# Routed attention of four batches in 32-row groups, in a two-layer language tower on one core

## The reference

```python
scores = sigmoid(normed @ Wr + br)
k = max(1, int(round(0.15 * l)))               # 19 of 128 tokens of a batch
_, idx = top_k(-scores, k)
attn_mask = zeros((b, l), bool).at[arange(b)[:, None], idx].set(True)
...                                            # 12-head attention of all tokens
attn_out = ctx @ Wo + bo
...
merged = where(attn_mask[..., None], attn_out, mix_out)
h = hidden_states + merged
```

## Time and profile before

| | |
|---|---|
| time, median of 3 runs | 887.48 us (884.51 to 888.21) |
| span of the profiled execution | 888.4 us |
| PE busy | 722.9 us (81%), 5500 instructions |
| DVE busy | 519.8 us (59%), 1760 instructions |
| ACT busy | 302.3 us (34%) |
| POOL busy | 245.1 us (28%) |
| chain that ended last, by engine | PE 61%, DVE 18%, issue 6%, POOL 4%, ACT 4%, DMA 3% |
| mean granted clock of TensorE | 0.931 of full speed |

### The profile page before, as it was taken

The page is one execution under the profiler, slowest core; times in us unless marked ns, Lnnn a source line. Parts: engine busy times, 40 slices in busy tenths (PEclk is TensorE's granted clock), DMA queues, the critical chain, the costliest instruction groups (busy, mean ns, idle before and its releaser), DMA issues.

```text
span 888.4 us, 15579 instructions
## 1 busy us (share of the span) xinstructions
PE 722.9 (81%) x5500; PEld 545.4 (61%) x5501; DVE 519.8 (59%) x1760; ACT 302.3 (34%) x688; POOL 245.1 (28%) x304
## 2 busy tenths in 40 slices
PE   1888778988777998858798967768868879999993
PEld 1546355566556665647656645745447878988892
DVE  7458677865678774668887367871253443333330
ACT  0133241634333253433353433421334323333330
POOL 5322200470013244001445201330001533333332
PEclk9999899999968999998999997889897989999997
DMA  7950000000001000000111000048001323222220
GB/s 249 412 237 2 0 1 1 19 7 2 1 1 37 23 17 4 2 1 1 54 19 8 1 3 1 25 173 284 0 2 31 63 49 46 36 36 38 36 35 8
DMA packets 29894, 43.63 MB, mean 49 GB/s; under 512 B 5355, under 2 KB 24597, under 8 KB 29830
## 3 DMA queue, kind: packets, MB, share of 16 engines
q1 hardware_dynamic: 19250, 30.87, 10.1%
q0 software_dynamic: 8752, 9.07, 6.3%
q10 hardware_dynamic: 1828, 2.84, 0.9%
HBM read 21.36 MB, written 22.09 MB: 49 GB/s over the span
## 4 chain that ended last, share of the span: by engine, by line
PE 61%; DVE 18%; issue 6%; POOL 4%; ACT 4%; DMA 3%; another core or an unknown queue 1%; ACTq 1%; SPq 1%; DVEq 0%; POOLq 0%
PE qa L1840 26%; PE qc L1840 25%; PE qa L1843 5%; PE qc L1843 4%; DMA out<-qk_T 2%; DVE mx L1435 2%; POOL arena_w L440 1%; DMA mu_row<-in_mu 1%; DVE st L1042 1%; POOL rs_a L475 1%; ACTq L633 1%; DVE arena_e L1256 1%; DVE qk_T L1441 1%; DVE xb L1059 1%
## 5 line engine op out<-in xcount | busy, mean ns | idle before, releaser
L1840 PE MATMUL qc<-arena_w,big 128*128 x468 | 83.1, 328 | 1.4 <-DVE qk_T L1819 1.4
L1840 PE MATMUL qa<-arena_b 128*128 128x128 f32 (+2 forms) x688 | 75.1, 293 | 9.7 <-ACT arena_b L763 4.9
L1840 PEld LDWEIGHTS qa<-arena_b 128*128 128x128 f32 (+2 forms) x688 | 66.1, 195 | 19.4 <-issue 7.5
L1840 PEld LDWEIGHTS qc<-arena_w,big 128*128 128x128 f32 x468 | 75.6, 191 | 2.1 <-issue 2.0
L1008 ACT ACTIVATE big<-qa,arena_b 128x128 f32<-128x128 f32 x156 | 43.1, 375 | 80.8 <-PE qc L1840 66.9
L1840 PE MATMUL qa<-arena_e,nT 128*128 128x192 f32 (+2 forms) x256 | 69.9, 429 | 0.4 <-ACT nT L671 0.3
L1808 DVE COPY arena_b<-qc 128x256 f32<-128x256 f32 x39 | 16.6, 426 | 90.6 <-PE qc L1843 79.6
L603 POOL DMA_INDIRECT out<-qk_T x39 | 61.1, 1566 | 21.0 <-POOL spare L602 10.6
L1840 PEld LDWEIGHTS qa<-arena_e,nT 128*128 128x128 f32 x256 | 47.0, 198 | 22.0 <-issue 12.3
L475 POOL TENSOR_TENSOR rs_a<-rs_a,minus_half 128x4 f32<-128x4 f32 x8 | 8.1, 1012 | 177.5 <-DVE rs_a L1055 170.1
L479 POOL TENSOR_TENSOR rs_b<-rs_b,minus_half 128x4 f32<-128x4 f32 x12 | 12.5, 1042 | 152.3 <-DVE rs_b L1055 152.3
(11 more groups left out here) (368 smaller groups left out, 1592.0 us busy)
## 6 DMA issues: line engine op xcount, KB each, us to landing
slots<-xk SPq DMA_DIRECT2D x1, 13192.0 KB, 43.1
arena_e<-in_w SPq DMA_DIRECT2D x8, 579.0 KB, 7.9
arena_w<-in_w SPq DMA_DIRECT2D x8, 576.0 KB, 9.0
qk_T<-slots SPq DMA_DIRECT2D x39, 97.0 KB, 1.9
out<-hb SPq DMA_DIRECT2D x16, 96.0 KB
arena_e<-in_w_l SPq DMA_DIRECT2D x1, 804.0 KB
arena_e<-in_W ACTq DMA_DIRECT2D x1, 768.0 KB
out<-qk_T POOLq DMA_INDIRECT x39
```

What stands on the lines that cost most here:

```text
L1840: return nc.tensor.matmul(o, l, r, start=start, stop=stop)
```

## The change

The 19 selected tokens of the four batches are laid side by side, each padded to a group of 32 (KP = 32), so that the four batches fill 128 rows.

```diff
-        pw = sb("pw", [128, G, KSEL + 1])
+        pw = sb("pw", [128, G, KP])
-        ctxT = sb("ctxT", [KR, C, G, KSEL])
+        ctxT = sb("ctxT", [KR, C, G, KP])
+        def attn_of(b):
+            return QA[:, (b + 2) % G, 0:D]
...
             def pselT_evac(ta):
-                w(ta, "pselT_p", 4)
-                A(pselT[:, :, :].rearrange("p b t -> p (b t)"), PA[0:KSEL, 0, :], ACT.Copy).then_inc(*done("pselT"))
+                w(ta, "pselT_p", 1)
+                A(pselT, PA[:, 0, 0:128], ACT.Copy).then_inc(*done("pselT"))
-            def asel_evac(ta, hf):
-                w(ta, "asel_p", 2 * hf + 2)
-                A(aselb[:, 2 * hf:2 * hf + 2, :].rearrange("p b n -> p (b n)"), PB[0:KSEL, hf, 0:2 * D], ACT.Copy).then_inc(*done("asel"))
+            def asel_evac(ta):
+                w(ta, "asel_p", 1)
+                A(aselb, PB[:, 0, 0:D], ACT.Copy).then_inc(*done("asel"))
...
-            step(fill(ctxT[CW:KR, :, :, :], 0.0))
+            step(fill(ctxT[:, :, :, :], 0.0))
+            step(fill(pw[:, :, :], 0.0))
...
             def contexts(ta, hf):
-                for b in (2 * hf, 2 * hf + 1):
-                    w(ta, "ctx", half(b))
-                    T(ctxm[:, :, b, :].rearrange("p c (h k) -> p c h k", h=HC),
-                      half_of(PB, CW, b // 2, HC * KSEL)[:, b % 2, :, :].rearrange("p c (h k) -> p c h k", h=HC),
-                      bc(bc(hmb, 2, KSEL), 1, C), ALU.mult).then_inc(s["ctx_m"], 1)
-                    w(ta, "ctx_m", b + 1)
-                    nc.vector.reduce_sum(ctxT[0:CW, :, b, :], ctxm[:, :, b, :].rearrange("p c (h k) -> p c k h", h=HC),
-                                         AX.X).then_inc(s["ctxT"], 1)
+                two = slice(2 * hf, 2 * hf + 2)
+                w(ta, "ctx", 2 * hf + 2)
+                T(ctxm[:, two, :, :].rearrange("p b c (h k) -> p (b c) h k", h=HC),
+                  half_of(PB, CW, hf, HC * KSEL).rearrange("p b c (h k) -> p (b c) h k", h=HC),
+                  bc(bc(hmb, 2, KSEL), 1, 2 * C), ALU.mult).then_inc(s["ctx_m"], 1)
+                w(ta, "ctx_m", hf + 1)
+                nc.vector.reduce_sum(ctxT[0:CW, :, two, 0:KSEL].rearrange("p c b k -> p b c k"),
+                                     ctxm[:, two, :, :].rearrange("p b c (h k) -> p b c k h", h=HC), AX.X).then_inc(s["ctxT"], 1)
             def selected_in(ta, hf):
                 for b in (2 * hf, 2 * hf + 1):
-                    w(ta, "attn", half(b))
+                    w(ta, "attn", b + 1)
                     w(ta, "hin", b + 1)
-                    T(x[:, b, :], x[:, b, :], psl(PB, b, D), ALU.add).then_inc(s["hin"], 1)
+                    T(x[:, b, :], x[:, b, :], attn_of(b), ALU.add).then_inc(s["hin"], 1)
...
             def x1_T(ta, hf):
-                since(pe, s["hin"], ta * PER["hin"] + (2 * hf - 2))
+                since(pe, s["hin"], ta * PER["hin"] + (hf - 3))
             def proj(ta, b):
                 w(ta, "xT", 1 if b == 0 else 2)
+                if b == 0:
+                    since(pe, s["hin"], ta * PER["hin"])
...
             def select_T(ta):
                 w(ta, "rank", 20)
-                for b in range(G):
-                    inc(tr(PA[0:KSEL, 0, tok(b)], pw[:, b, 0:KSEL], 128), "pselT_p")
+                inc(tr(PA[:, 0, 0:128], pw[:, :, :].rearrange("p b k -> p (b k)"), 128), "pselT_p")
...
-            def selected(ta, hf):
-                w(ta, "ctxT", 2 * hf + 2)
-                for b in (2 * hf, 2 * hf + 1):
-                    inc(both(psl(PB, b, D)[0:KSEL, :], lambda c: ctxT[:, c, b, :], lambda c: w_fo[:, c, :]), "asel_p")
-            def attn(ta, hf):
-                w(ta, "asel", hf + 1)
-                for b in (2 * hf, 2 * hf + 1):
-                    inc(mm(psl(PB, b, D), pselT[:, b, :], aselb[:, b, :]), "attn")
+            def selected(ta):
+                w(ta, "ctxT", 2)
+                inc(both(PB[:, 0, 0:D], lambda c: ctxT[:, c, :, :].rearrange("p b k -> p (b k)"), lambda c: w_fo[:, c, :]), "asel_p")
+            def attn(ta):
+                w(ta, "hin", G)
+                w(ta, "asel", 1)
+                for b in range(G):
+                    rows_ = slice(KP * b, KP * b + KSEL)
+                    inc(mm(attn_of(b), pselT[rows_, :], aselb[rows_, :]), "attn")
```

More of the change, by code:

```diff
@@ L30 @@
 KSEL = max(1, int(round(0.15 * S)))
+KP = 32
 NE = 8
@@ L71 @@
     ln2=15, ln3=7, zdot=4, zexp=1, score=7, n3T=4, nT=2, dg=4, bc=4, ssum=1, bcs=1, rank=22,
-    sel=4, selT=2, qT=1, q_bias=2, kT=1, kT_evac=2, v2p=4, v2=2, pselT_p=4, pselT=1, lg=4, nmax=8,
-    pexp=8, pnorm=12, pT_p=4, pT=2, ctx=4, ctx_m=4, ctxT=4, asel_p=4, asel=2, attn=4, mixT=8, mix=4, hin=8, hb=8,
+    sel=4, selT=2, qT=1, q_bias=2, kT=1, kT_evac=2, v2p=4, v2=2, pselT_p=1, pselT=1, lg=4, nmax=8,
+    pexp=8, pnorm=12, pT_p=4, pT=2, ctx=4, ctx_m=2, ctxT=2, asel_p=1, asel=1, attn=4, mixT=8, mix=4, hin=8, hb=8,
     ln4=15, n4T=4, n2T=2, up=6, gelu=6, down=4, h_ffn=4,
@@ L159, in build @@
         qbd = part(arena_w, over, [C, G, HC * KSEL], CW)
-        ctxm = part(arena_w, over, [C, G, HC * KSEL], CW)
-        aselb = part(arena_w, over, [G, D], KSEL)
-        pselT = part(arena_w, over, [G, 128], KSEL)
+        ctxm = part(arena_w, over, [G, C, HC * KSEL], CW)
+        aselb = part(arena_w, over, [D])
+        pselT = part(arena_w, over, [128])
         assert over[0] <= at[0]
@@ L343, in build @@
         KC = (97, 96)
-        V_EMPTY, V_TAU = 2, 25
-        V_MQK, V_UM = 26, 27
-        V_SETUP = 39
+        V_EMPTY, V_TAU = 2, 26
+        V_MQK, V_UM = 27, 28
+        V_SETUP = 40
         R_EARLY, R_DONE = 23, 43
@@ L869, in front @@
                 pT_evac(ta, 1)
-                asel_evac(ta, 0)
-                asel_evac(ta, 1)
+                asel_evac(ta)
             def joint(ta, tb):
@@ L1992, in select @@
                     for c in range(C):
-                        i = mm(PA[0:CW, c, lo:lo + KSEL + 1], xn[:, b, c * CW:(c + 1) * CW], pw[:, b, :])
+                        i = mm(PA[0:CW, c, lo:lo + KSEL + 1], xn[:, b, c * CW:(c + 1) * CW], pw[:, b, 0:KSEL + 1])
                     inc(i, "sel")
@@ L2235, in front @@
                 context(ta, 1)
-                selected(ta, 0)
-                selected(ta, 1)
-                attn(ta, 0)
-                attn(ta, 1)
+                selected(ta)
+                attn(ta)
             def joint(ta, tb):
```

## The result

| | before | after |
|---|---|---|
| median, us (lowest to highest, runs) | 887.21 (884.35 to 888.21, 6) | 890.2 (889.74 to 891.71, 6) |
| ratio after/before, 95% interval | | 1.0047 [1.0034, 1.006] |
| span of the profiled execution, us | 888.4 | 887.9 |
| mean granted clock in it | 0.931 | 0.911 |

The changed kernel is 0.47% slower, 3.0 us between these medians, and the forecast of 885.2 with its range up to 889.0 missed it. The two profiled spans seem to say the opposite. In every run whose span is known the time is the span plus 1.8 to 1.9 us, so the profile of before came from a long execution (its time would be 890.3). The kernel before ran 98 times more beside the experiments, in four rounds with medians of 886.15 to 886.98, at a clock of 0.923 to 0.932 (one more run, of 1109.12 us, is left out).

What follows compares the result with a forecast made beforehand. At the ends of the front and turns, VectorE was taken as nearly the bound. Savings of 1.2 + 0.95 + 0.77 + 0.46 = 3.4 us, less 1.1 for a clock fall, gave net 2.3: 885.2 us, range 881.8 to 889.0.

Steps and rivals of the forecast that it cites:

- The sum: Savings at the four ends before any clock loss: 1.2 + 0.95 + 0.77 + 0.46 = 3.4 us (2.3 to 4.5).
- The back products: Four products spreading contexts back over tokens; even run serially they were in time under VectorE's work, so overlap costed at nothing.
- C: End of a turn at about 444 us; saving 0.46 + 0.31 = 0.77 us.
- at B, C and D only the second pair counts: At these ends a quicker first mask pair only waits for TensorE, so only the second pair's 0.27 us saving counts.
- B: End of a turn at about 298 us, TensorE at its lower clock; saving taken as 0.95 us (0.6 to 1.1).
- D: Turn 3 into the back, about 590 us; saving 0.46 us only, since the statistics need all of x.
- A: Front into turn 1, about 148 us; saving 0.18 + 0.5 + 0.53 = 1.2 us.
- I expect a fall at C that was not there, price 1.1; A and B keep theirs.: TensorE's clock falls newly at C, costing 1.1 us; the low stretches at A and B stay as they were.
- The third rival: Projections at A, B and C start and stay at low clock, costing 4.85 us: 889.0, chance 0.15.
- The kind clock: C stays at full clock, turn 1's low time shortens by a third: 3.4 + 1.6 = 5.0 us, 882.5, chance 0.25.
- No gain: Slow reduction and late back products leave `selected_in` unmoved; 1.1 us saved less 0.6 for clock: 887.0, chance 0.15.
- The reading against the median: Whole kernel: profiled span 888.4 us against median 887.48, called slow by 0.9; forecast 886.1 on the span, 885.2 against median.

Runs made afterwards that it cites:

- e1: The changed kernel with unread TensorE products in three gaps at the end of the front and of each turn; 886.38 us, ratio to before 0.9992.
- e5: The kernel before with no edit, run again for a second profile; profiled span 884.1 us, clock 0.929.
- e11: e3 with unread products: three behind the last context product, a half one behind the Wo product and behind the back products; 882.96 us, ratio 0.9967.
- e2: The kernel before with only the two-batch masks and reductions, its TensorE work unchanged; 883.77 us, ratio 0.9977.
- e12: e1 with three unread products instead of two behind the last context product; 886.29 us, ratio 0.9988.
- e3: The changed kernel with masks and reductions of one batch each, as before, TensorE part of the change kept; 904.46 us, ratio 1.0204.
- e6: e1 with more unread products in each joint turn: one ahead of the queries, two ahead of the mix; 884.16 us, ratio 0.9984.
- e8: The changed kernel with unread products in one place only, two behind the last context product; 886.71 us, ratio 1.0009.
- e9: e2 with unread products in each joint turn: one ahead of the queries, two ahead of the mix; 885.77 us, ratio 0.999.

## Why the prediction was wrong

**The sum is borne out as far as it can be seen.** The forecast's sum of 3.4 us before any clock stands against 3.5 at equal low time, which is good to a us or two. Its terms: mask 0.62 to 0.63 (taken 0.62), reduction 0.92 to 0.93 (taken 0.93), evacuation 0.33 (bound 0.48), the Wo product 0.92 at full clock (taken 0.78). The back products overlap almost fully, 0.61 us for eight where one row group took 1.56, and at full clock they are hidden, as costed. C was put at 0.77 and measures 0.9 (7.4 to 6.5). The first mask pair may count too: "at B, C and D only the second pair counts" rested on the extra 1.3 us of lag of one execution. The shares of A, B and D were not measured singly. The forecast's working for B reads 3.94 us as the sixteen product instructions "and attn"; the row is the sixteen alone, and the 0.25 each is right for them.

**The step that failed** is "I expect a fall at C that was not there, price 1.1; A and B keep theirs." The fall at C came, with the mechanism named. The term of 1.1 us was mis-sized: the runs show 32 us of extra low time, which is some 7.4 us at 0.23 per us (6.7 to 9.3 at 0.21 to 0.29), though not all of it can be laid to the thinned stretch: with the gaps filled 9 to 10 us of it stay. Three things in that sentence were wrong.

- Where: it comes at every end. The chain has 12.94, 12.19 and 13.11 for the three projections. B had no standing fall to keep: its low `context(1)` (1.48) is in one of five profiles with the TensorE work of before. A has one in three of the five (12.18, 12.50, 12.50 against 10.80 twice), so "keeps" was fair for A, though the fall grew there.
- How long: I priced the stretch of the projections alone. The trace of after has these stretches at the low level around the ends (start + length, us; the last column is the whole profile), beside both profiles of before and e1:

```text
          A            B            C                          D             all
before    147.2+3.4    290.6+3.4    none                       591.0+10.2    125.3
e5        133.4+6.8    none         none                       594.2+10.2    128.2
after     145.4+6.8    295.6+6.8    435.5+3.4, 445.7+10.2      595.9+13.7    161.0
e1        none         none         none                       590.6+10.2    134.7
```

  Of the 32.8 us that after has more than e5, 23.9 stand in this table; most of the other 9 lie earlier in the turns. Those and the one at 435.5, which is over before `context(1)` of C, are not in the thinned stretch, and no run ties them to it.

- Through what: the low level reaches the short chain itself. At C the Wo product, the back products and the transposes take 0.73, 0.41 and 0.86 us more than in e1, and the cover of the back products, costed at nothing, is gone: VectorE waits 1.01 for them.

**The third rival** ("the clock turns on the change") is the one that came true in mechanism, with all three ends low. It was under-sized in low time: 15.5 us of extra low time, the difference between two turns of one execution, where 32 came. Its price of 0.31 per us was somewhat high (0.21 to 0.29 between kernels, 0.25 within before). It gave 889.0 with a chance of 0.15; with 32 us at 0.23 on the forecast's 3.4 it gives 887.5 - 3.4 + 7.4 = 891.5, and 890.2 was measured. What should have raised its chance stood in the working: some 2.3 us taken out of 3.83 busy in 4.25, in the one stretch where nothing else can run, and the same edit at all four ends.

The section "HAM oscillation — how this bites in real kernels" of the Trainium skill (TensorE: Matmul & The Clock Gate) says that bursts between idle gaps each start cold; I weighed it down because in the trace of before only the thin stretch at A was followed by a low clock. For the changed kernel's ends the trace agrees in kind (0.62 and 13.11 at C). The waits in its example are longer than the 1.68 us that TensorE idled here at most in that stretch, and the clock fell all the same.

**The kind clock** (882.5) did not come with this kernel, but e11 and e2 reach about that, with 124.2 and 122.5 us of low time. Its sum takes a third of the 4.85 us between the turns (1.6); a third of turn 1's low time, as its text has it, is 10 us (0.10 x 2 x 150.42 / 3), which at 0.31 gives 3.1 and 881.0. **No gain** (887.0) is not borne out: `selected_in` starts 4.8 us behind the end of `context(1)` in e1 and 5.4 in e5, and the filled kernels are faster at equal low time; in after the gain is there and is outweighed.

**The reading against the median** was wrong in its base. The profile was called slow by 0.9 us; by its span it was slow by 3 to 4 against typical runs. The scale of net gains was kept, so this moved the number little, but it is where the low clock of B and the lag came from.

**Open.** With the ends filled, the kernels with two-batch masks stay at 137 us of low time while e11, with one-batch masks, is at 124; e12 has runs of both kinds, 880.6 and 887. In the profiles of e3, e6 and e8 the first expert tiles ran 34 to 38 us on end at the low level, in after and e5 about 10 of the same 34, so some of the spread in low time has nothing to do with the ends. Why a run takes the one or the other was not settled. What caused the lag in the first profile of before is not known either.

## What to carry to other kernels

Before you take work off an engine that is hidden anyway, ask what that work did for TensorE's clock: in the stretch ahead of a large burst, a small product under another engine's shadow can be worth more than it costs, as the sixteen product instructions at the ends were here. Price such an edit at two clock levels over the stretch and all that follows, not over the next instructions alone, and test it by putting unread products in the gap, which cost little when the gap is real. Take a second profile of the same kernel before building on which places are low: here the first profile showed a lag and a low clock at B that no other profile of the same TensorE work has, and a low clock at A that three of five have.

## What the hardware showed that I had not expected

- Unread products, twenty of them, bring 904.46 down to 882.96 us.
- A microsecond at the lower clock costs 0.21 to 0.29 us of the whole. That much of TensorE's time is off the path (PE has 61% of the chain of before) is the likely reason; no run tests it.
- Executions of one unchanged program differ by up to 17 us of low time (120 to 137), and with fillers by more (121 to 155 in e6, 111 to 149 in e9).
- Products whose 19 rows lie in different groups of 32 rows and write different banks overlap: 0.61 us for eight instructions of 192 columns, 1.56 without.
- A VectorE reduction of 96 x 456 in float32 takes 0.93 us, and one of 96 x 228 takes 0.54: the doubling saves 0.15.
- The first copy behind a group of transposes started 1.95 to 2.10 us after them in one profile of the kernel before and 0.65 in another of the same program.
